# Attentions of 96-wide heads: half of the output projection's first four chunks stands in the gaps of the last heads, and squares stand directly behind each chunk

## The reference, cut to what matters

```python
q = q.reshape(n, H, DH) * DH ** (-0.5)
scores = jnp.einsum('nhd,mhd->hnm', q, k)
probs = jax.nn.softmax(scores, axis=-1)
attn = jnp.einsum('hnm,mhd->nhd', probs, v).reshape(n, D)
attended = attn @ Wo.T + bo
return nodes + attended
```

```python
q_norm = jnp.sum(q * q, axis=-1, keepdims=True) * 0.5
phi_q = jnp.exp(jnp.einsum('bhnd,md->bhnm', q, rf) - q_norm)
kv = jnp.einsum('bhnm,bhnd->bhmd', phi_k, v)
numerator = jnp.einsum('bhnm,bhmd->bhnd', phi_q, kv)
attn = numerator / jnp.maximum(denominator, 1e-06)
return out @ proj_w.T + proj_b
```

## Time and profile before

| | us |
|---|---|
| median of 3 runs | 4366.4 |
| lowest and highest | 4365.52, 4368.17 |
| the profiled execution | 4363.68 |
| its span | 4362.0 |
| TensorE busy in it | 4137.1 (95%) |
| VectorE, ScalarE busy | 1153.9, 951.3 |

### The profile page before, as it was taken

The page is one execution under the profiler, slowest core; times in us unless marked ns, Lnnn a source line. Parts: engine busy times, 40 slices in busy tenths (PEclk is TensorE's granted clock), DMA queues, the critical chain, the costliest instruction groups (busy, mean ns, idle before and its releaser), DMA issues.

```text
span 4362.0 us, 37147 instructions
## 1 busy us (share of the span) xinstructions
PE 4137.1 (95%) x14783; PEld 1958.6 (45%) x14801; DVE 1153.9 (26%) x2082; ACT 951.3 (22%) x1743; POOL 137.5 (3%) x220
## 2 busy tenths in 40 slices
PE   8999999999999988989999999988999999999998
PEld 5444444444445444444454545434444333343333
DVE  7884221213221425113410111215530000000000
ACT  2121112434224336222200000116420100111000
POOL 2022000000000000000000000000000000000000
PEclk9999999999999999999999999999999999999999
DMA  5945422110741210103212122390159999999998
GB/s 194 295 138 155 122 85 80 37 44 22 288 186 44 68 58 1 61 27 134 72 55 92 61 84 69 128 368 25 53 205 424 406 422 416 423 423 404 424 410 358
DMA packets 170561, 802.34 MB, mean 184 GB/s; under 512 B 51898, under 2 KB 69114, under 8 KB 123812
## 3 DMA queue, kind: packets, MB, share of 16 engines
q1 hardware_dynamic: 158356, 733.39, 44.6%
q0 software_dynamic: 9584, 47.06, 2.8%
q10 hardware_dynamic: 2464, 19.67, 1.1%
HBM read 780.91 MB, written 71.10 MB: 195 GB/s over the span
## 4 chain that ended last, share of the span: by engine, by line
PE 83%; DMA 6%; DVE 5%; ACT 4%; issue 1%; POOL 0%; SPq 0%; DVEq 0%; ACTq 0%; POOLq 0%
PE bank L714 76%; DMA mem<-in_experts 4%; PE bank L875 3%; PE bank L712 2%; PE bank L849 1%; DMA mem<-moe_up 1%; ACT mem L1920 1%; DVE mem L2611 0%; ACT mem L1956 0%; ACT mem L1941 0%; ACT mem L2093 0%; DVE mem L2607 0%; DVE mem L2389 0%; DVE mem L2388 0%; DVE mem L2282 0%
## 5 line engine op out<-in xcount | busy, mean ns | idle before, releaser
L714 PE MATMUL bank<-mem 128*128 128x512 f32 (+4 forms) x10296 | 3161.8, 553 | 56.5 <-DMA mem<-in_experts 25.5
L714 PEld LDWEIGHTS bank<-mem 128*64 128x64 f32 (+2 forms) x10296 | 1330.8, 166 | 1788.2 <-issue 1675.6
L712 PE MATMUL bank<-ident,mem 128*128 128x128 f32 (+2 forms) x1484 | 228.7, 304 | 76.6 <-ACT mem L2120 14.8
L712 PEld LDWEIGHTS bank<-ident,mem 128*128 128x128 f32 (+2 forms) x1484 | 188.8, 157 | 169.6 <-issue 88.0
L1553 ACT ACTIVATE mem<-bank,cols 128x512 f32<-128x512 f32 x66 | 45.3, 687 | 760.7 <-PE bank L714 760.7
L875 PE MATMUL bank<-mem 128*128 128x512 bf16 x798 | 177.9, 382 | 3.5 <-DVE mem L2389 2.5
L2990 DVE TENSOR_TENSOR mem<-mem,EV 128x512 f32<-128x512 f32 x48 | 33.2, 692 | 550.0 <-ACT EV L2194 550.0
L2968 DVE TENSOR_TENSOR mem<-mem,bank 128x512 f32<-128x512 f32 x48 | 33.0, 688 | 456.3 <-PE bank L714 456.3
L714 PE MATMUL bank<-mem,ones 128*128 128x512 f32 (+1 forms) x290 | 128.3, 611 | 17.7 <-ACT mem L1587 7.2
L875 PEld LDWEIGHTS bank<-mem 128*128 128x128 bf16 x816 | 79.7, 98 | 101.4 <-DVE mem L2389 4.2
L1553 ACT ACTIVATE mem<-bank 128x512 f32<-128x512 f32 x81 | 47.7, 596 | 248.8 <-PE bank L714 244.0
(11 more groups left out here) (401 smaller groups left out, 2560.9 us busy)
## 6 DMA issues: line engine op xcount, KB each, us to landing
mem<-in_experts SPq DMA_DIRECT2D x282, 1536.0 KB, 12.0
mem<-in_weights SPq DMA_DIRECT2D x285, 512.0 KB, 3.5
mem<-moe_up SPq DMA_DIRECT2D x30, 1152.0 KB, 9.6
mem<-moe_down SPq DMA_DIRECT2D x30, 1152.0 KB, 11.1
moe_up<-in_weights SPq DMA_DIRECT2D x16, 1152.0 KB
moe_down<-in_weights SPq DMA_DIRECT2D x16, 1152.0 KB
mem<-head_tiles SPq DMA_DIRECT2D x36, 384.0 KB, 3.0
mem<-in_weights POOLq DMA_DIRECT2D x36, 384.0 KB, 7.6
```

The costliest lines, as they stand in the source:

```text
L712: ins = nc.tensor.transpose(out, lhsT, ident[0:lhsT.shape[0], 0:lhsT.shape[0]])
L714: ins = nc.tensor.matmul(out, lhsT, rhs, start=start, stop=stop)
```

## The change

The first three of the six matmuls (input chunks 0 to 2) of the output projection's chunks 0 to 3 are issued before head 7 is done, into banks 4 to 7 (`early_half`). The other three of each follow behind the last head (`late_half`); chunks 4 and 5 stay with `linear` and the banks in turn. In the softmax attention chunks 0 and 1 stand in head 6's gap between scores and transposes and chunks 2 and 3 in head 7's. In performer96 chunk 0 stands in head 6's gap between the key features and `m_kv`, chunk 1 in head 7's, and chunks 2 and 3 behind head 7's `m_out`. An early half takes its weight tile and keeps it until the late half. The late halves signal `agg_done`, ScalarE signals `act_done` when it has moved them, and VectorE waits for that.

Also, in performer96 ScalarE now squares a chunk's own head directly behind moving that chunk, the queries before the keys have arrived. The split heads 3 and 7 are squared in the gaps of heads 2 and 6 as before.

```diff
+SOFT_EARLY = {6: (0, 1), 7: (2, 3)}
+MIX_EARLY = {6: (0,), 7: (1,)}
+EARLY_OUT = 4
...
+            def early_half(label, m, ready):
+
+                slot = take_tile()
+                state["early", m] = slot
+                if m == 0:
+                    ready(0)
+                for k in range(KC // 2):
+                    mm(bank[4 + m][:, :], ring[:, slot, k * P:(k + 1) * P], att[:, k, :], k == 0, False)
+
+            def late_half(label, m, ready):
+
+                if m == 0:
+                    ready(KC // 2)
+                for k in range(KC // 2, KC):
+                    ins = mm(bank[4 + m][:, :], ring[:, state["early", m], k * P:(k + 1) * P], att[:, k, :], False, k == KC - 1, k == KC - 1)
+                state["pending"] = tile_free
+                ins.then_inc(agg_done.sem, agg_done.tick((label, m)))
...
+                    for m in SOFT_EARLY.get(h, ()):
+                        early_half("wo", m, attended)
                     pe.wait_ge(dve_done.sem, dve_done.at(("probs", h)))
...
-                linear("wo", KC, WHOLE, of(att), lambda k: pe.wait_ge(bank_free.sem, bank_free.at(("att", 4 * (k // 3) + 3))))
+                for m in range(EARLY_OUT):
+                    late_half("wo", m, attended)
+                linear("wo", KC, WHOLE, of(att), first=EARLY_OUT)
...
+                    for m in MIX_EARLY.get(h, ()):
+                        early_half("proj0", m, attended)
                     pe.wait_ge(bank_free.sem, bank_free.at(("m_phi_k", h, 1)))
...
-                linear("proj0", KC, WHOLE, of(att), lambda k: pe.wait_ge(dve_done.sem, dve_done.at(("m_att", 4 * (k // 3) + 3))))
+                for m in range(2, EARLY_OUT):
+                    early_half("proj0", m, attended)
+                for m in range(EARLY_OUT):
+                    late_half("proj0", m, attended)
+                linear("proj0", KC, WHOLE, of(att), first=EARLY_OUT)
...
-            def residual(label, bias=None):
+            def residual(label, bias=None, early=0):
 
                 for m in range(KC):
-                    act.wait_ge(bank_full.sem, bank_free.now(1))
-                    src = filled()
+                    if m < early:
+                        act.wait_ge(agg_done.sem, agg_done.at((label, m)))
+                        src, evicted = bank[4 + m], act_done
+                    else:
+                        act.wait_ge(bank_full.sem, bank_free.now(1))
+                        src, evicted = filled(), bank_free
...
+                    squares(own, (kind,))
+
+                def squares(h, kinds):
...
-                squares(0)
...
-                    if h + 1 < H8:
-                        squares(h + 1)
+                    if h in (2, 6):
+                        squares(h + 1, (0, 1))
```

More of the change, by code:

```diff
@@ L750, in take_x_tile, with linear @@
                 return t % XRING
-            def linear(label, n_out, tiles, moving, ready=None, width=P, extra=None, squares_of=None):
+            def early_half(label, m, ready):
[12 more added lines that the diff above has]
+                ins.then_inc(agg_done.sem, agg_done.tick((label, m)))
+            def linear(label, n_out, tiles, moving, ready=None, width=P, extra=None, squares_of=None, first=0):
                 total = sum(n for n, _ in tiles) + (extra is not None)
-                for m in range(n_out):
+                for m in range(first, n_out):
                     out = open_bank()[0:width, :]
@@ L899, in softmax_attention @@
                 v_tok = tokens(B_)
+                attended = lambda k: pe.wait_ge(bank_free.sem, bank_free.at(("att", 4 * (k // 3) + 3)))
                 linear(("aq", 0), 1, WHOLE, of(chunks(A_)))
@@ L942, in performer96 @@
             def performer96():
+                attended = lambda k: pe.wait_ge(dve_done.sem, dve_done.at(("m_att", 4 * (k // 3) + 3)))
                 linear(("mq", 0), 1, WHOLE, x_n)
@@ L1564, in residual @@
                     nc.scalar.activation(EV[:, m % 2, :], src[:, :], ACT.Identity, **how).then_inc(
-                            bank_free.sem, bank_free.tick((label, m)))
+                            evicted.sem, evicted.tick((label, m)))
                     ev_reader[m % 2] = (label + "_x", m)
@@ L1706, in softmax_attention @@
                                 bank_free.sem, bank_free.tick(("att", h)))
-                residual("wo", bias_of("L0_gnn_bo"))
+                residual("wo", bias_of("L0_gnn_bo"), EARLY_OUT)
             def performer96():
@@ L1722, in queries_or_keys @@
                                          bias=split_bias(1, kind, i), scale=s).then_inc(bank_free.sem, bank_free.tick(((name, i), 0)))
-                def squares(h):
+                    squares(own, (kind,))
+                def squares(h, kinds):
                     own, i = mix_own(h), head_chunk(h) if h % 4 < 3 else 3 * (h // 4) + 2
-                    act.wait_ge(bank_free.sem, bank_free.at((("mk", i), 0)))
-                    for kind in range(2):
+                    for kind in kinds:
+                        act.wait_ge(bank_free.sem, bank_free.at(((("mq", "mk")[kind], i), 0)))
                         nc.scalar.activation(own[0:D8, 2 + kind, :], own[0:D8, kind, :], ACT.Square).then_inc(
@@ L1777, in performer96 @@
                             bank_free.sem, bank_free.tick(("m_out", h)))
-                residual("proj0", bias_of("L0_mix_proj_b"))
+                residual("proj0", bias_of("L0_mix_proj_b"), EARLY_OUT)
             def experts_of_one(tag, ln, func):
@@ L2289, in times_rstd, with residual @@
                     v.tensor_tensor(x[:, m, :], x[:, m, :], rstd[:, :], ALU.mult).then_inc(dve_done.sem, dve_done.tick((label, m)))
-            def residual(label, full=None, before=None):
+            def residual(label, full=None, before=None, early=0):
                 for m in range(KC):
-                    dve.wait_ge(bank_free.sem, bank_free.at((full or label, m)))
+                    evicted = act_done if m < early else bank_free
+                    dve.wait_ge(evicted.sem, evicted.at((full or label, m)))
                     v.tensor_tensor(XT[:, m, :], XT[:, m, :], EV[:, m % 2, :], ALU.add).then_inc(
@@ L2436, in softmax_attention @@
                 for m in range(KC):
-                    dve.wait_ge(bank_free.sem, bank_free.at(("wo", m)))
+                    evicted = act_done if m < EARLY_OUT else bank_free
+                    dve.wait_ge(evicted.sem, evicted.at(("wo", m)))
                     v.tensor_tensor(EV[:, m % 2, :], EV[:, m % 2, :], chunks(A_)[:, m, :], ALU.add).then_inc(
@@ L2470, in performer96 @@
                                 dve_done.sem, dve_done.tick(("m_att", h)))
-                residual("proj0", before="ln1")
+                residual("proj0", before="ln1", early=EARLY_OUT)
             def experts_of_one(tag, ln):
```

## The result

| | before | changed |
|---|---|---|
| median of 5 runs, us | 4367.14 | 4347.31 |
| lowest and highest | 4365.52, 4373.0 | 4346.69, 4351.83 |
| profiled execution, span | 4363.68, 4362.0 | 4346.69, 4345.1 |

The ratio is 0.9957, with a 95% interval of 0.9946 to 0.9967: 14 to 24 us off, 19.8 between the medians. Forecast were 16.85 us, to 4349.6.

The account below looks back on a forecast made before the run. TensorE, 83% of the chain, was taken as the bound. Softmax 9.7 + squares 2.9 + performer96 5.9 - one clock fall 1.65 = 16.85 us off, 4346.8 for the profiled execution, 4349.6 for plain runs; range 4344 to 4357.

Parts of the forecast that it names:

- What bounds it: Both attentions: TensorE is 83% of the chain that ended last, so time is won where it stands still or is slow.
- Head 6: Softmax attention: transposes start at 872.02 us without the 3.86 us wait, take about 2.0 us, values start at 874.0.
- The transposes' rule: Softmax gaps of heads 6 and 7: by the skill's rule the clock is at risk, gain 5.5 us; head 5's row preferred.
- The new wait: Behind softmax head 7: TensorE stands about 2.1 us before the late halves, until ScalarE's three moves are done.
- Squares: performer96's norms: squaring the query earlier starts TensorE 0.58 us sooner five times, 2.9 us gained; bounds 0 and 2.9.
- performer96's projection: Early halves in gaps and behind `m_out`: gain 5.9 us if the clock stays up behind a 2.7 us stop, otherwise 4.2.
- The clock behind the stops: Behind the 2.1 and 2.7 us stops: each a toss, one fall of two counted, costing about 1.65 us.
- The low clock in the gaps: Rival, softmax heads 6 and 7: clock stays low, both stops fall, gain 10.95 us, time 4355.4; chance 0.12.
- the squares for nothing: Rival, performer96: `m_kv`'s result, not the square, ends the wait; gain 13.95 us, time 4352.4; chance 0.09.
- a tile or bank that waits: Rival, inside the gaps: a late half waits for its tile or a bank; gain 8.4 us, time 4358; chance 0.04.
- the rest got slower: Rival, behind the attentions: 16 more clock falls at later stops cost 26.4 us, time 4376; chance 0.03.
- the sign I had named for it: Sign of a wrong forecast: a span behind the attentions that differs by more than 3 us from before.

Follow-up runs that it names:

- e4: Changed kernel with one early half in each softmax gap and two behind head 7; head 5's last transposes to next layer norm's sums 226.51 us, changed kernel 227.35.
- e5: Changed kernel with the first three matmuls of chunk 4 of both projections ahead of the late halves; 4344.09 us, ratio to the kernel before 0.9939.
- a0: The changed kernel again, unaltered, in a second comparison; 4354.09 us, ratio to the kernel before 0.9965.
- a1: The changed kernel a third time, unaltered; single time 4351.04 us.
- b1: The kernel before the change, run once more unaltered; single time 4373.8 us.
- e2: Kernel before plus only the softmax attention's early halves, squares in old order; head 5's last transposes to next layer norm's sums 234.33 us, before 246.26.
- e1: Kernel before plus only the new order of squares, both projections unsplit; head 5's last transposes to next layer norm's sums 244.92 us, before 246.26.
- e3: Kernel before plus only performer96's early halves, squares in old order; head 5's last transposes to next layer norm's sums 242.08 us, before 246.26.
- e6: As e5, with ScalarE squaring a chunk's own head before moving split rows, and split head 3 before head 2's fill; 4342.12 us, ratio to before 0.9938.
- a2: The changed kernel a fourth time, unaltered; single time 4348.85 us.

## Why the prediction was right, point by point

- *What bounds it.* Right: of the 14.1 us that TensorE waited before in the places that the early halves were to fill (3.86 and 0.69 twice each, 4.99), 4.3 are left (1.90 and 2.41).
- *Head 6.* Forecast 872.02 for the transposes, from heads 2 and 3; measured 872.01. The values followed 1.74 us behind, not 2.0, and again in head 7 (885.77 to 887.52). That is 0.5 us of the 0.6 by which this part was under-sized: 10.31 without a fall, against 9.7. Another 0.1 is a slip: 891.5 + 0.2 + 1.8 + 0.1 is 893.6, not 893.7.
- *The transposes' rule.* The full clock through both gaps (e4 too, with 1.29 us of waiting) bears out the row I took. The Trainium skill ("TensorE: Matmul & The Clock Gate", Part 4: PE-mode transpose) doesn't count a transpose as busy in the way of a matmul; at this length nothing came of it, the granted clock was 1.00 through all 16 transposes.
- *The new wait.* 1.90 us, forecast 2.1, released as said. e5 shows that it was avoidable.
- *Squares.* 2.6 instead of 2.9: a square standing alone takes 0.63 us, not half of the 1.15 of an overlapping pair, so each wait shrank by 0.52. The one of 1.49 (forecast 1.5) came as said.
- *performer96's projection.* 6.0 without a fall, forecast 5.9 (from the norms at 1047.29 before and 1034.39 changed to the sums: 58.20 and 52.19 us); each gap's delay was 1.62, not 1.75, and the stop 2.41, not 2.7.
- *The clock behind the stops.* One fall of the two: right in number, four times of four, and its price too, 1.7 against 1.65. With one toss each I could as well have met none or both, so the number was luck, or a link between the stops that I didn't have. By the rule of the Trainium skill ("TensorE: Matmul & The Clock Gate", "A second HAM failure mode: psum-queue depth-cycling") I had both falls due; the runs show one. The page speaks of frequent short stops between groups, here two stand 171 to 173 us apart, so its rule was a poor fit.
- *The term I missed.* The low clock at head 0's features, 1.7 us, was in the trace before, and the forecast doesn't mention it, so it put its change at nothing. All four executions of the changed kernel were free of it. With 10.3 + 2.6 + 6.0 - 1.7 + 1.7 = 18.9 the stretch closes; forecast were 16.85. The projection's last move, forecast between 1087 and 1090, came at 1086.78, just ahead of that, by this term. The medians of the plain runs moved 19.8 in one comparison and 14.2 in the other; they can't tell 16.85 from 18.9.
- *Rivals.* The low clock in the gaps, the squares for nothing, a tile or bank that waits: none was seen. That the rest got slower was not seen either. But the sign I had named for it, a span behind the attentions more than 3 us off, was too narrow to mean anything: it was 8.5 and 5.7 us off in a0 and a1, and 10.2 us off in the kernel before itself (b1). The 2.65 us between three runs, on which I had leaned, were too few runs to show how far the time moves.

## What to carry to other kernels

When a sum's early terms are ready long before its late ones, split it and put the early part where the matrix engine waits for others; it costs spare banks and weight buffers held longer, and here both were free. Count what the moved part used to hide: the first half of chunk 0 had covered ScalarE's last moves, and keeping one more half in that place, in both projections (e5), was worth another 6.4 us. To judge a change of some microseconds in a long program, measure between two rows that both traces share: the stretch repeated within 0.03 us here, while the untouched rest moved by 10. It did so because each of the four traces held exactly one fall; where their number changes, it moves by 1.7 us a fall. And when an experiment lands outside what was expected of it, as e2 did by 0.9 us, look for the term behind it: here the clock at a place further on whose code was the same.

## What the runs showed of the hardware that was not expected

- The same stops in the same kernel fall or not from execution to execution, yet exactly one of two stops 171 to 173 us apart did, four times of four. That is too few to show a link; one execution's trace can't tell which stop it will be.
- Whether the clock was down at head 0's features was the same in every trace of a kernel where there is more than one, behind an equal wait of 1.79 us: down in both traces before (3.54 us), in e1 (3.04), e3 (3.46) and e6 (3.60); up in all four of the changed kernel and in e2, e4 and e5 (1.98 or 1.99). It was down in every kernel whose first projection stood unsplit and up in all with early halves there but e6. What sets it was not settled.
- A fall cost nearly the same at different places: 1.7 us at either stop in the four traces of the changed kernel (from the stop to the projection's last move 22.6 us against 20.9) and 1.7 us at head 0's features (5.25 us against 3.55). One was dearer: in e1 from the stop of 4.98 us to the last move it was 31.44 us, before 30.16. The time to the first move alone (4.13 us in a2, 4.58 in the first trace, against 2.88) can give part of the price only.
